# A Mamba block with its feed-forward layer on one core: two output products moved behind the last masked product, the first half's statistics on ScalarE, the bias added by GpSimd

## The chip, the cores and the metric

The kernel runs on one core of one Trainium2 chip. The metric is the device time of one launch in microseconds (us), as the median of several runs. Before the change it is 1815.36 us.

## What is computed

The input is x, 1024 tokens by 512 channels, in float32. A row of six vectors (shift, scale and gate, twice) comes from a small conditioning product. Cut to what matters here:

```python
h = layernorm(x) * (1 + ca) + sa
x = x + ga * attn(h)          # Mamba-2: in_proj, conv, SSD over 128 heads, group norm, out_proj
h = layernorm(x) * (1 + cb) + sb
x = x + gb * (h @ sign(w_ffn).T + b_ffn)
```

In `attn`, the 8192 inner channels are normalised in 8 groups of 1024: `g = y * silu(gate)`, divided by the root of the mean of g squared over the group, then multiplied with `out_proj_w` and summed over all groups.

## The kernel before, in words

**Tiles and units.** Tokens are worked on in two halves of 512 (four chunks of 128). Inner channels are worked on in 16 blocks of 512 (8 heads). A unit is one block for one half. There are 32 units, numbered u; four of them (c = 0 to 3) make a group g, in the order block 0 half 0, block 0 half 1, block 1 half 0, block 1 half 1. The last unit (g = 7, c = 3, `end` in the code) is followed by a tail: the output products of the last unit, the second layernorm, and the feed-forward product.

**Order of work.** Everything is written out by hand in five instruction streams (SyncE, TensorE, ScalarE, VectorE, GpSimd), with semaphores between them; the program order of each engine is the order of the code. No scheduler moves anything.

**One unit.** TensorE makes the gate projection, transposes the convolved x (`transposes`, L745), makes chunk states (`states`, L667), and, in the first part of unit u, the output products of unit u-1 (`out_proj(u - 1, z)`, four of them, z = 0 to 3, each of 12 matmuls 128x512 on lines 492 to 494, into banks 4 and 5 in turn). Then come four steps j, of two heads each: `exp_a` (L698) and `diff` (L681) are the products that ScalarE turns into decays (L1137, L1129, L1132); VectorE multiplies the decays with the masked C·B matrix (`mix`, L1517); TensorE makes Y_off (L819) and the masked product Y_diag (L836); VectorE adds the skip and scales Y_off (L1542, L1547); GpSimd adds and gates (L1734, L1737); ScalarE rounds the gated tile to its high part and squares it (`split_g`, L1149, L1156); VectorE makes the low part (`lower_g`, L1524); GpSimd sums the squares (`add_squares`, L1729). The last masked product is L836 of j = 3.

**Output products and the accumulator.** VectorE's `accumulate` reads an output product from its bank and adds the partial sum that a DMA brought (L1430), in the last unit and the tail multiplies by the gate row ga (L1433), and adds it, scaled by the group's inverse root, to `acc`, the residual stream (L1439). The products of u = 30, made in the last unit, complete the first half of `acc` (tiles 0 to 3). The products of u = 31, made in the tail, complete tiles 4 to 7.

**The second layernorm and the feed-forward layer.** At the end of the last unit VectorE takes mean and variance of tiles 0 to 3 (L1275, L1277) ahead of its last `lower_g`. In the tail ScalarE normalises (`normalise`, L1222), TensorE transposes (`turn`, L862), ScalarE scales and shifts the transposed tile and rounds it (`to_h`, L1242, L1244), VectorE makes the low part (`low`, L1591). The statistics of tiles 4, 5 and 6 are two passes on ScalarE (`stats`, L1227, L1229), those of tile 7 VectorE's. For each token tile t TensorE adds the bias as two products of one row (`bias`, L867, L868) and makes eight matmuls (`ffn`, L873); VectorE multiplies by gb and adds to `acc` (`y`, L1598, L1600); SyncE stores the tile.

The program prints the functions that the change touches here:

## Time and profile before

| what | value |
|---|---|
| median of 3 runs | 1815.36 us (1815.17 to 1816.68) |
| the profiled execution's own time | 1818.66 us |
| its span, first to last instruction | 1816.8 us |
| TensorE busy | 1744.9 us, 96% |
| VectorE busy | 1287.3 us, 71% |
| ScalarE busy | 1026.3 us, 56% |
| GpSimd busy | 946.0 us, 52% |
| mean granted TensorE clock | 0.989 of full speed |

Times in the trace are microseconds from the start of the span. A row of a timeline gives the start, the duration, the engine, the line, the operation, the tile written and the tiles read; in square brackets, how long the engine had been idle before it and which instruction ended that. "x2" means two such instructions merged in one row. Matmuls overlap, so one row's duration is longer than the distance to the next.

### The profile page before, as it was taken

The numbers are of one execution on the slowest core, as the hardware profiler recorded it, in microseconds if no ns is written. First come the engines' busy times: TensorE is split into PE (matmuls) and PEld (weight loads), VectorE is DVE, ScalarE is ACT, GpSimd is POOL, SyncE is SP. The second block draws the span as 40 slices with busy tenths as digits, with TensorE's granted clock in tenths as the row PEclk, the third lists the DMA queues.
The fourth block names the chain that finished last, engine by engine and source line by source line (L and its number), as shares of the span: only waits on it lengthen the run. The fifth ranks groups of instructions, "written<-read, shape, count | busy, mean of one in ns | idle before, by whom it ended". The sixth has DMA issues, their size and how long they took to land.

```text
span 1816.8 us, 31172 instructions
## 1 busy us (share of the span) xinstructions
PE 1744.9 (96%) x9672; PEld 1331.0 (73%) x9672; DVE 1287.3 (71%) x2154; ACT 1026.3 (56%) x1732; POOL 946.0 (52%) x732
## 2 busy tenths in 40 slices
PE   6889999999999999999999999999999999999968
PEld 4567778777777777777777777777777777877756
DVE  4766677767766678766777677666787667876776
ACT  6556555665546556565555655465564655556544
POOL 1445464555535565354645555455653546666651
PEclk9899999999999999999999999999999999999989
DMA  6312121121212121021211212121210212212111
GB/s 228 105 35 73 56 71 47 44 61 54 73 29 73 50 71 52 26 73 56 69 50 37 67 49 79 29 73 48 67 58 27 73 56 67 71 49 67 56 47 58
DMA packets 80789, 112.44 MB, mean 62 GB/s; under 512 B 28385, under 2 KB 32481, under 8 KB 79842
## 3 DMA queue, kind: packets, MB, share of 16 engines
q1 hardware_dynamic: 62754, 77.71, 14.5%
q10 hardware_dynamic: 17856, 32.51, 5.3%
q8 instruction: 91, 1.49, 0.4%
q14 instruction: 88, 0.72, 0.1%
HBM read 87.90 MB, written 22.29 MB: 61 GB/s over the span
## 4 chain that ended last, share of the span: by engine, by line
issue 48%; POOL 35%; PE 9%; ACT 3%; DVE 2%; DMA 1%; SPq 1%; POOLq 1%; ACTq 0%; DVEq 0%
POOL yt L1734 10%; POOL ssq L1729 7%; POOL prev L1713 5%; POOL wg_lo L1639 4%; POOL wo_lo L1639 3%; POOL yt L1737 3%; POOL wx_lo L1639 2%; PE bank L492 2%; PE bank L494 2%; PE bank L493 2%; PE bank L667 1%; PE bank L873 1%; PE bank L745 1%; POOL acc L1659 1%; POOL acc L1657 0%
## 5 line engine op out<-in xcount | busy, mean ns | idle before, releaser
L1734 POOL TENSOR_TENSOR yt<-yt,ea 128x384 f32<-128x384 f32 (+1 forms) x128 | 189.5, 1480 | 386.4 <-DVE ea L1547 386.4
L1517 DVE TENSOR_TENSOR lm<-lm,cbm 128x512 f32<-128x512 f32 x256 | 189.4, 781 | 161.5 <-ACT lm L1132 161.4
L1328 DVE SCALAR_TENSOR_TENSOR xc<-bank,bpar,xc 128x511 f32<-128x511 f32 (+2 forms) x384 | 286.2, 745 | 6.8
L492 PE MATMUL bank<-h_hi,wg_hi 128*128 128x512 f32 x640 | 262.7, 410 | 21.3 <-ACT gate L1078 11.1
L494 PE MATMUL bank<-h_hi,wg_lo 128*128 128x512 f32 x640 | 251.5, 393 | 0.0
L493 PE MATMUL bank<-h_lo,wg_hi 128*128 128x512 f32 x640 | 250.5, 391 | 0.0
L492 PE MATMUL bank<-h_hi,wx_hi 128*128 128x512 f32 x512 | 211.3, 413 | 2.3 <-DVE bt L1328 2.3
L492 PE MATMUL bank<-wo_hi,g_hi 128*128 128x512 f32 x496 | 206.6, 417 | 0.0
L494 PE MATMUL bank<-h_hi,wx_lo 128*128 128x512 f32 x512 | 201.7, 394 | 0.0
L493 PE MATMUL bank<-h_lo,wx_hi 128*128 128x512 f32 x512 | 200.7, 392 | 0.0
L494 PE MATMUL bank<-wo_hi,g_lo 128*128 128x512 f32 x496 | 194.8, 393 | 0.0
L1713 POOL TENSOR_TENSOR prev<-prev,dec 128x512 f32<-128x512 f32 x96 | 102.2, 1064 | 175.4 <-DVE prev L1471 110.2
L493 PE MATMUL bank<-wo_lo,g_hi 128*128 128x512 f32 x496 | 193.3, 390 | 0.0
L1078 ACT ACTIVATE gate<-bank 128x512 f32<-128x512 f32 x128 | 75.2, 587 | 207.2 <-PE bank L494 83.6
L1137 ACT ACTIVATE ea<-bank 128x512 f32<-128x512 f32 x128 | 76.5, 598 | 187.6 <-PE bank L698 139.9
L1737 POOL TENSOR_TENSOR yt<-yt,gate 128x512 f32<-128x512 f32 x128 | 165.6, 1294 | 10.0
L492 PEld LDWEIGHTS bank<-h_hi,wg_hi 128*128 128x128 f32 x640 | 120.8, 189 | 64.3 <-DVE xc L1328 14.6
L948 ACT ACTIVATE xc<-bank,bpar 128x512 f32<-128x512 f32 (+1 forms) x128 | 99.2, 775 | 112.9 <-PE bank L494 63.5
L1132 ACT ACTIVATE lm<-lm 128x512 f32<-128x512 f32 x256 | 148.9, 644 | 0.0
L1639 POOL TENSOR_TENSOR wx_lo<-raw_w,wx_hi 128x512 fp32r<-128x512 f32 x64 | 87.3, 1369 | 118.4 <-ACT wx_hi L918 118.4
L836 PE MATMUL bank<-lm,xdt 128*64 128x128 f32 x2048 | 140.9, 280 | 4.0 <-DVE lm L1517 2.0
L1729 POOL TENSOR_TENSOR ssq<-ssq,sq 128x512 f32<-128x512 f32 x112 | 144.4, 1290 | 0.0
(210 smaller groups left out, 3712.7 us busy)
## 6 DMA issues: line engine op xcount, KB each, us to landing
raw_w<-w_in_dram SPq DMA_DIRECT2D x145, 256.0 KB, 2.7
raw_w<-w_out_dram SPq DMA_DIRECT2D x64, 256.0 KB, 2.6
part_d<-part ACTq DMA_DIRECT2D x64, 256.0 KB, 2.4
part<-part_d ACTq DMA_DIRECT2D x60, 256.0 KB, 2.7
rt<-rows_d SPq DMA_DIRECT2D x256, 6.0 KB
acc<-x_dram SPq DMA_DIRECT2D x8, 256.0 KB, 6.6
acc<-w_mod_dram SPq DMA_DIRECT2D x2, 1024.0 KB, 6.0
lh<-neg_d SPq DMA_DIRECT2D x128, 6.0 KB
```

Source lines behind the costliest of these rows:

```text
L492: nc.tensor.matmul(out_ap, whi(k), hhi(k), start=(k == 0), stop=False)
L493: nc.tensor.matmul(out_ap, whi(k), hlo(k), start=False, stop=False)
L494: last = nc.tensor.matmul(out_ap, wlo(k), hhi(k), start=False, stop=(k == n - 1))
L836: lst = nc.tensor.matmul(bank[yd_bank(end, j)][64 * i:64 * i + 64, chunk(z)], xdt[:, z, h * HDIM:(h + 1) * HDIM], lm[:, h % 4, chunk(z)], ...
L1132: act(lm[:, h % 4, :], lm[:, h % 4, :], ACT.Exp, scale=-1.0).then_inc(a_l, 1)
L1328: stt(dst[:, at], ps[:, 0:HALF - 3 + k], w(k), dst[:, at], ALU.mult, ALU.add)\
L1517: tt(lm[:, h % 4, :], lm[:, h % 4, :], cbm[:, toks(hf)], ALU.mult).then_inc(v_m, 1)
L1639: tt(lo[:, j, :], raw_w[:, s, :], hi[:, j, :].bitcast(F), ALU.subtract).then_inc(p_w, 1)
L1713: tt(prev[:, slot(hf, z + 1), :].rearrange("p (h c) -> p h c", h=BH), prev[:, slot(hf, z), :].rearrange("p (h c) -> p h c", h=BH), d.unsqu ...
L1729: tt(ssq[:, hf, :], ssq[:, hf, :], sq[:, :], ALU.add).then_inc(p_ss, 1)
L1734: tt(yt[:, j % 2, cols], yt[:, j % 2, cols], ea[:, j % 2, cols], ALU.add).then_inc(p_t3, 1)
L1737: tt(yt[:, j % 2, :], yt[:, j % 2, :], gate[:, j, :], ALU.mult).then_inc(p_g, 1)
```

## The change

It has five parts, all in the last unit and the tail.

1. **Output products.** In the last unit TensorE makes `out_proj(30, 2)` and `out_proj(30, 3)` behind the last masked product, not ahead of the first decays. VectorE's `accumulate` for them moves with them: z = 2 stands behind its last L1547 and ahead of the low part of j = 2, z = 3 ahead of the low part of j = 3. SyncE's loads of the partial sums wait for these.
2. **First half's statistics.** VectorE's four means and variances at the end of the last unit are gone. ScalarE makes them in two passes per tile (`stats(0)` to `stats(3)`): two tiles between its work for j = 2 and for j = 3, two behind j = 3. VectorE scales the sums in one small instruction in the tail (`variance`), behind the group's sum. Tiles 6 and 7 are VectorE's now (`own_stats`), tiles 4 and 5 remain ScalarE's.
3. **Tail order.** TensorE transposes tiles 0 to 3 behind `out_proj(31, 2)`, where it was behind `out_proj(31, 1)`. VectorE adds the third accumulator tile ahead of the first two low parts, and the fourth, with `own_stats(6)` and `own_stats(7)`, ahead of the other two. ScalarE normalises tiles 4 to 7 behind all four `to_h` of the first half. The feed-forward product of tiles 0 and 1 is interleaved by k, as that of 4 and 5 already was.
4. **Bias.** The two one-row products per token tile are gone. GpSimd multiplies the bias, loaded to all 128 partitions, by gb once in the last unit, and adds it to each tile of `acc` when that tile has been normalised (`add_bias`); VectorE's last addition waits for it. The two ScalarE copies that split the bias row are gone.
5. **Squares.** In the last unit the squares of odd j go to a buffer of their own, and GpSimd adds those of j = 1 and j = 2 behind the gating of j = 3.

The core of the diff:

```diff
 TensorE, last unit
                     if z == 3:
-                        if not first:
+                        if not first and not end:
                             out_proj(u - 1, 2, None, (g, c))
                         states(2)
                         exp_a(0)
                         diff(0)
                         diff(1)
-                    if not first:
+                    if not first and not (end and z == 3):
 TensorE, tail
+            te.wait_ge(a_ea, 4 * UNITS)
+            out_proj(u - 1, 2, None, (GROUPS - 1, 3))
+            te.wait_ge(v_t2, 4 * u + 3)
+            out_proj(u - 1, 3, None, (GROUPS - 1, 3))
+            out_read(GROUPS - 1, 3, 2)
             out_proj(u, 0, None, (GROUPS, 0))
             sum_squares(GROUPS - 1, 1)
+            out_read(GROUPS - 1, 3, 3)
             out_proj(u, 1, None, (GROUPS, 0))
+            out_proj(u, 2, None, (GROUPS, 0))
             te.wait_ge(a_fall, 8 * UNITS)
             for t in range(NZ):
                 turn(t)
-            out_proj(u, 2, None, (GROUPS, 0))
             out_proj(u, 3, None, (GROUPS, 0))
-            te.wait_ge(p_bias, 1)
...
+            ffn_tiles(0, 1)
+            te.wait_ge(ln_sems[1]["a_n"], NK)
+            turn(4)
+            turn(5)
+            out_read(GROUPS, 0, 2)
+            ffn_tiles(2)
+            turn(6)
+            turn(7)
+            out_read(GROUPS, 0, 3)
+            ffn_tiles(3)
+            te.wait_ge(v_y, 2)
+            ffn_tiles(4, 5)
+            te.wait_ge(v_y, 3)
+            ffn_tiles(6)
+            te.wait_ge(v_y, 4)
+            ffn_tiles(7)
 ScalarE
+            def stats(t):
+                se.wait_ge(v_acc, 4 * (UNITS - 2) + t + 1)
+                act(xw[:, 0, :], acc[:, t, :], ACT.Identity, scale=-1.0 / HID, accum_out=nmr[:, t:t + 1]).then_inc(a_st, 1)
+                se.wait_ge(a_st, 2 * t + 1)
+                act(xw[:, 1, :], acc[:, t, :], ACT.Square, bias=nmr[:, t:t + 1], accum_out=mv[:, t, 1:2]).then_inc(a_st, 1)
...
+                    if j == 3 and not more:
+                        se.wait_ge(t_st, states_before(NBLK, 0))
+                        stats(0)
+                        stats(1)
 VectorE, last unit
+                    if end and j == 3:
+                        accumulate(u, g1, b1, h1, 2, end)
                     if j >= 1:
                         lower_g(j - 1)
...
                 if end:
-                    for t in range(NZ):
-                        ve.wait_ge(v_acc, 4 * (UNITS - 2) + t + 1)
-                        token_stats(ln_sems[1], t, acc_tile)
...
-                    half_var(ln_sems[1], 0)
+                    accumulate(u, g1, b1, h1, 3, end)
                 lower_g(NCT - 1)
 GpSimd
+            def add_bias(t):
+                po.wait_ge(a_xn, t + 1)
+                tt(acc[:, t, :], acc[:, t, :], bias_row, ALU.add).then_inc(p_bias, 1)
+            norm_pair(slice(0, NZ), 1)
+            po.wait_ge(p_gbias, 1)
+            add_bias(0)
+            norm_pair(slice(4, 5), 2)
+            for t in range(1, NZ):
+                add_bias(t)
+            norm_pair(slice(5, 6), 3)
+            po.wait_ge(v_neg, 1)
+            norm_pair(slice(6, 7), 4)
+            po.wait_ge(v_neg, 2)
+            norm_pair(slice(7, 8), 5)
+            for t in range(NZ, NT):
+                add_bias(t)
```

Line numbers of VectorE's instructions shift with the change (L1430, L1433, L1439 become L1445, L1448, L1459, and L1524 becomes L1544).

The first place is VectorE at the end of the last unit. `bank0` and `bank7` are the two products of j = 3; `wx_lo` holds the low parts of the gated tiles of this unit; `part` and `acc` are those of `accumulate`. Before:

```order
L1542 SCALAR_TENSOR_TENSOR yt<-xc,bpar,bank0 128x512
L1547 TENSOR_TENSOR ea<-bank7,ea 128x512
L1524 SCALAR_TENSOR_TENSOR wx_lo<-yt,bpar,wx_hi 128x512
L1275 BN_STATS bn<-acc 128x6
L1277 BN_AGGR mv<-bn 128x2
```

The pair of L1275 and L1277 stands there four times, and after it two small instructions and the last low part. With the change:

```order
L1562 SCALAR_TENSOR_TENSOR yt<-xc,bpar,bank0 128x512
L1567 TENSOR_TENSOR ea<-bank7,ea 128x512
L1445 TENSOR_TENSOR part<-bank4,part 128x512
L1448 TENSOR_TENSOR part<-part,rows 128x512
L1459 SCALAR_TENSOR_TENSOR acc<-part,rstd,acc 128x512
L1544 SCALAR_TENSOR_TENSOR wx_lo<-yt,bpar,wx_hi 128x512
L1445 TENSOR_TENSOR part<-bank5,part 128x512
L1448 TENSOR_TENSOR part<-part,rows 128x512
L1459 SCALAR_TENSOR_TENSOR acc<-part,rstd,acc 128x512
L1544 SCALAR_TENSOR_TENSOR wx_lo<-yt,bpar,wx_hi 128x512
```

The four statistics are gone, and the two accumulations stand one ahead of each of the last two low parts.

The second place is ScalarE at the end of the last unit, from the high part of j = 2 to the normalising of the first half. Before:

```order
L1149 ACTIVATE wx_hi<-yt,bpar 128x512 [waits p_g]
L1156 ACTIVATE sq<-yt 128x512 [waits p_ss]
L1149 ACTIVATE wx_hi<-yt,bpar 128x512 [waits p_g]
L1156 ACTIVATE sq<-yt 128x512 [waits p_ss]
L1222 ACTIVATE xc<-acc,nmr,rs 128x512 [waits p_nmr,v_t2]
```

With the change:

```order
L1158 ACTIVATE wx_hi<-yt,bpar 128x512 [waits p_g]
L1169 ACTIVATE sq<-yt 128x512 [waits p_ss]
L1100 ACTIVATE xw,nmr<-acc 128x512 [waits v_acc,t_st]
L1102 ACTIVATE xw,mv<-acc,nmr 128x512 [waits a_st]
L1100 ACTIVATE xw,nmr<-acc 128x512 [waits v_acc]
L1102 ACTIVATE xw,mv<-acc,nmr 128x512 [waits a_st]
L1158 ACTIVATE wx_hi<-yt,bpar 128x512 [waits p_g]
L1169 ACTIVATE ssq<-yt 128x512 [waits p_ss]
```

Two tiles' statistics stand ahead of the last high part; the other two follow the last row shown.

The third place is VectorE in the tail, ahead of the third and fourth low part of the first half (`h_lo`). Before:

```order
L1430 TENSOR_TENSOR part<-bank4,part 128x512
L1433 TENSOR_TENSOR part<-part,rows 128x512
L1439 SCALAR_TENSOR_TENSOR acc<-part,rstd,acc 128x512
L1591 TENSOR_TENSOR h_lo<-lm,h_hi 128x512 x2
L1581 TENSOR_SCALAR rs<-mv 128x1
```

With the change:

```order
L1445 TENSOR_TENSOR part<-bank5,part 128x512
L1448 TENSOR_TENSOR part<-part,rows 128x512
L1459 SCALAR_TENSOR_TENSOR acc<-part,rstd,acc 128x512
L1594 TENSOR_SCALAR rs<-mv 128x1
L1284 BN_STATS bn<-acc 128x6
L1286 BN_AGGR mv<-bn 128x2
L1601 TENSOR_SCALAR nmr<-mv 128x1
L1602 TENSOR_SCALAR rs<-mv 128x1
```

The last four of these stand there twice, and then come the two `h_lo`: the fourth accumulation (`bank5`) and both tiles' statistics are now ahead of them, where only the third accumulation was.

## Rows read from the trace of the kernel before

**Rows 1.** The page: span, and TensorE's busy time.

```profile
span 1816.8 us, 31172 instructions
PE 1744.9 (96%) x9672; PEld 1331.0 (73%) x9672; DVE 1287.3 (71%) x2154; ACT 1026.3 (56%) x1732; POOL 946.0 (52%) x732
```

**Rows 2.** Stretches: start:end, length, each engine's busy us, PEclk, DMA share.

```profile
1760.40:1769.90 9.50, 0.07 (x2) 0.00 (x0) 7.42 (x16) 2.88 (x5) 8.91 (x7) 0.69 0.01 2
1769.90:1774.00 4.10, 4.03 (x10) 3.20 (x11) 0.01 (x1) 2.76 (x4) 2.33 (x3) 0.50 0.00 0
...
1785.80:1798.80 13.00, 11.98 (x48) 8.08 (x47) 8.07 (x17) 6.81 (x13) 3.18 (x6) 0.87 0.11 42
```

**Rows 3.** Who waited for whom, 1725 to 1817: total, times, longest.

```profile
PE bank L492 <- DVE wx_lo L1524: 9.5, 1, 9.5
```

**Rows 4.** Timeline of TensorE: start, duration, instruction.

```profile
1742.12 0.50 PE L492 MATMUL bank<-wo_hi,g_hi 128*128 128x512 f32 x1
...
1759.37 1.09 PE L836 MATMUL bank<-lm,xdt 128*64 128x128 f32 x16 [1.37 <-DVE lm L1517]
1769.97 0.80 PE L492 MATMUL bank<-wo_hi,wx_hi 128*128 128x512 f32 x1 [9.50 <-DVE wx_lo L1524]
...
1775.59 0.47 PE L492 MATMUL bank<-wo_hi,wx_hi 128*128 128x512 f32 x1
...
1778.45 1.91 PE L862 MATMUL bank<-ident,xc 128*128 128x128 f32 x16
...
1785.77 0.49 PE L867 MATMUL bank<-wg_hi 1*128 1x512 f32 x1
...
1797.79 1.03 PE L862 MATMUL bank<-ident,prev 128*128 128x128 f32 x8
...
1810.16 0.49 PE L867 MATMUL bank<-wg_hi 1*128 1x512 f32 x1
...
1810.82 0.50 PE L873 MATMUL bank<-wg_lo,h_hi 128*128 128x512 f32 x1
```

**Rows 5.** Timeline of VectorE.

```profile
1741.05 0.69 DVE L1430 TENSOR_TENSOR part<-bank,part 128x512 f32<-128x512 f32 x1 [1.70 <-PE bank L494]
...
1747.67 1.29 DVE L1517 TENSOR_TENSOR lm<-lm,cbm 128x512 f32<-128x512 f32 x2
...
1750.29 2.36 DVE L1517 TENSOR_TENSOR lm<-lm,cbm 128x512 f32<-128x512 f32 x2
...
1764.50 0.98 DVE L1524 SCALAR_TENSOR_TENSOR wx_lo<-yt,bpar,wx_hi 128x512 fp32r<-128x512 f32 x1 [1.78 <-ACT wx_hi L1149]
1765.40 0.68 DVE L1275 BATCH_NORM_STATS2 bn<-acc 128x6 f32<-128x512 f32 x1
...
1788.62 0.69 DVE L1591 TENSOR_TENSOR h_lo<-lm,h_hi 128x512 fp32r<-128x512 f32 x1 [0.64 <-ACT h_hi L1244]
...
1813.67 0.69 DVE L1600 TENSOR_TENSOR acc<-acc,ea 128x512 f32<-128x512 f32 x1
```

**Rows 6.** Two lines of VectorE, 1570 to 1817: ns shortest/median/longest, first and last start.

```profile
L1430 DVE TENSOR_TENSOR part<-bank,part x12: 676/688/692, 1579.4 to 1789.3; 128x512 f32<-128x512 f32 x12
L1439 DVE SCALAR_TENSOR_TENSOR acc<-part,rstd,acc x12: 752/752/1723, 1580.7 to 1790.7; 128x512 f32<-128x512 f32 x12
```

**Rows 7.** Timeline of ScalarE.

```profile
1746.50 1.15 ACT L1132 ACTIVATE lm<-lm 128x512 f32<-128x512 f32 x2
...
1771.24 2.93 ACT L1222 ACTIVATE xc<-acc,nmr,rs 128x512 f32<-128x512 f32 x4 [1.41 <-POOL nmr L1746]
1778.17 0.63 ACT L1227 ACTIVATE ssq<-acc 128x512 f32<-128x512 f32 x1 [4.00 <-DVE acc L1439]
...
1780.07 0.78 ACT L1242 ACTIVATE lm<-bank,modc 128x512 f32<-128x512 f32 x1 [0.33 <-PE bank L862]
```

**Rows 8.** Timeline of GpSimd.

```profile
1750.30 1.80 POOL L1734 TENSOR_TENSOR yt<-yt,ea 128x512 f32<-128x512 f32 x1 [9.17 <-DVE ea L1547]
...
1767.90 1.27 POOL L1729 TENSOR_TENSOR ssq<-ssq,sq 128x512 f32<-128x512 f32 x1
```

More of the change, by code:

```diff
@@ L278, in ea_bank, with square @@
             return 4 if j else gate_bank(c, 2)
+        def square(end, j):
+            return ssq[:, 0, :] if end and j % 2 else sq[:, :]
         def yo_bank(end, j):
@@ L827, in unit @@
                         else:
-                            out_read(g, c, 3)
+                            out_read(g, c, 1 if end else 3)
                     else:
@@ L1497, in unit @@
                         tt(by_head(xw[:, z % 2, :]), src, heads(dtw[:, hf], 1, z), ALU.mult).then_inc(v_xw, 1)
-                    if z == 3 and not first:
-                        accumulate(u, g1, b1, h1, 2, end)
+                    if z == 3 and not first and not end:
+                        accumulate(u, g1, b1, h1, 2)
                     if z >= 1:
@@ L1528, in unit @@
                 mix(1)
-                if not first:
-                    accumulate(u, g1, b1, h1, 3, end)
+                if not first and not end:
+                    accumulate(u, g1, b1, h1, 3)
                 if hf == 0:
@@ L1728, in add_squares @@
                         ge(po, p_ss, squares_before(g, c) + j - (c < 2))
-                    tt(ssq[:, hf, :], ssq[:, hf, :], sq[:, :], ALU.add).then_inc(p_ss, 1)
+                    tt(ssq[:, hf, :], ssq[:, hf, :], square(last and c == 3, j), ALU.add).then_inc(p_ss, 1)
                 for j in range(NCT):
@@ L1737, in unit @@
                     tt(yt[:, j % 2, :], yt[:, j % 2, :], gate[:, j, :], ALU.mult).then_inc(p_g, 1)
-                    if j >= (2 if c < 2 else 1):
+                    if last and c == 3:
+                        for k in ((), (0,), (), (1, 2))[j]:
+                            add_squares(k)
+                    elif j >= (2 if c < 2 else 1):
                         add_squares(j - 1)
```

144 lines of the change are left out of this document (60 added, 84 removed).

## The prediction

> **What bounds the kernel now.** I read the page first: TensorE is busy 1744.9 of 1816.8 us [rows 1], so over 31 units it is the bound, and the change touches none of them. All of it lies behind 1738 us, so I read only that stretch, engine by engine. There TensorE is not the bound. Between its last masked product (L836, 1759.37 plus 1.09) and the first output product of u = 31 (1769.97) it does nothing for 9.5 us [rows 3, 4]: it waits for the last low part, L1524. Ahead of that stands a chain through all engines: VectorE's L1547, GpSimd's add and gate, ScalarE's high part, VectorE's low part. GpSimd is busy 8.91 of 9.50 us in this pause, VectorE 7.42 [rows 2]. After it the granted clock is 0.50 [rows 2], the lower of the two levels, for 4.1 us. The reader should see three milestones. **S** is the start of the first product of u = 31: 1769.97 [rows 4]. **L** is the end of the fourth low part of the first half: 1788.62 + 0.69 = 1789.31 [rows 5]. **T** is the end of the last transposes: 1797.79 + 1.03 = 1798.8 [rows 4]. Behind T a fixed chain runs to VectorE's last addition at 1813.67 [rows 5], and the store. I give each part as a shift of these.
>
> **The last unit's heads.** Removed: an output product is 12 matmuls, 1775.59 to 1778.45, 2.85 us [rows 4]. One stood ahead of the first decays, one from 1742.12 [rows 4] ahead of the second pair's. VectorE idled 1.70 us for the first one (1741.05) and spent about 2.1 us on each accumulation (0.69 + 0.69 + 0.75) [rows 5, 6]. Without them, ScalarE's own queue is next: its second pair of exponentials (1746.50 [rows 7]) can start when the first pair is done, which I put 2.9 us earlier. VectorE's second pair of masks (1747.67 [rows 5]) is then 3.4 us earlier, GpSimd's first add (1750.30 [rows 8]) too. In the middle steps some of it is lost to the next effect; the last masked product (1759.37) I put at 1756.25, 3.1 us earlier.
>
> **The end of the last unit, the largest term.** What L1517 shows is important: two masks take 1.29 us, but 2.36 us when GpSimd is adding (its L1734 from 1750.30 took 1.80, not 1.27) [rows 5, 8]. The low part at 1764.50 took 0.98 [rows 5]. L1430, which reads a bank, never takes over 692 ns, L1439, which reads two tiles, up to 1723 [rows 6]. So VectorE's instructions with two tiles as inputs and GpSimd's take turns. The Trainium skill, page "SBUF — State Buffer", section "SBUF: two separate sides", says so: a shared port pair is an exclusive lock for the whole instruction. The trace agrees, and it is a rule that speaks against this change. By that rule the sum below is as it stands; with no lock it would be the first rival's.
>
> From GpSimd's gating of j = 2, which ends at 1760.6 by the shifts above, there remain five GpSimd instructions of 1.25 us (add and gate of j = 3, three sums of squares; 1.27 in [rows 8] less the overlap) and, new, six of VectorE with two tiles, 0.62 each: two times multiply, accumulate, low part. Before, only two of these six stood there; the rest was statistics of one input (L1275, 0.68 [rows 5]). Taking turns: 5 x 1.25 + 6 x 0.62 = 9.95, so the low part ends at 1770.55 and S = 1770.65, **0.7 us later**. The 3.1 us are spent. Bounds: with no turns at all, ScalarE decides. High part of j = 2 to 1761.25, square 0.55, two tiles of statistics at 1.55 each (to 1764.9; L1227 is 0.63 [rows 7], and the other pass and the two reads bring it to 1.55), high part, low part: S = 1766.2. If the two moved products run at the lower clock (0.43 a matmul, 5.2 us each), the accumulations start later: S = 1771.3. I take the turns, because the rows show them at each overlap.
>
> **S to the fourth product.** Before 1769.97 to 1785.77, 15.8 us [rows 4], 1.8 us of them for the low clock behind the pause (nine matmuls 0.2 us slower). The pause is now 5.7 to 7.6 us, so I leave that in. The transposes, 1.91 us [rows 4], are only moved by one product: the fourth normalised tile comes just then. Again 15.85: **no shift**. But ScalarE's first `to_h` comes later. It was at 1780.07, S + 10.1 [rows 7]. Now: the group's sum at S + 5.6, VectorE's `variance` behind its first multiply at S + 6.4, GpSimd's two powers, four tiles in 2.93 [rows 7] to S + 11.7, `stats(4)` to S + 13.3, two `to_h` of 1.35 to S + 16.0.
>
> **The low parts in the tail.** L was S + 19.35. Now VectorE makes the second low part to S + 16.65, then accumulates the fourth tile (2.15), makes the statistics of tiles 6 and 7 (about 1.05 each: 0.68 [rows 5] and three small ones), and only then the third and fourth low part (1.3): S + 22.2. Beside it GpSimd makes three bias additions of 1.27 [rows 8], each of which can hold VectorE once; none to two full waits give 0 to 2.1, I take 1.0. L = S + 23.2, **3.85 us later** against S. Each accumulator addition also stands in front of its `own_stats`; TensorE, with its fourth product done and half of the two-tile product made, waits some 5 us for the third low part, and its clock can fall again.
>
> **L to T.** Before 9.5 us, with 3.4 us at the low clock (0.87 mean over 1785.8 to 1798.8 [rows 2]): two matmuls, a bias pair, eight matmuls, eight transposes, a bias pair, eight matmuls, eight transposes. Now four matmuls (1.0), eight transposes (1.03 [rows 4]), eight matmuls (2.1: from 1810.82 to the last addition's product [rows 4, 5]), eight transposes: 5.1 at the full clock, 6.6 if the pause brought it down. I take 5.9: **3.6 us earlier**.
>
> **Behind T.** The chain is `to_h`, low parts, y(3), low parts, then three tiles' products. Two bias pairs are on it, each 1810.82 - 1810.16 = 0.66 [rows 4]: **1.3 us earlier**. The four later bias additions of GpSimd are done before y needs them.
>
> **Edits that cost nothing.** The bias times gb on GpSimd (1.27) takes the place of the one-row subtraction, in the 9.17 us that GpSimd idles there [rows 8]; the bias load to all partitions has 25 us. The two copies that ScalarE loses stood in front of a wait for TensorE. If GpSimd's cover went, its first add would be 1.3 later at most.
>
> **Sum.** 0.7 + 0 + 3.85 - 3.6 - 1.3 = -0.35, with 0.05 for the longer 15.85: -0.3 us. On the profiled execution that is 1818.66 to 1818.4; its span is 1816.8 and 1.86 lie around it. The median is 3.3 below the profiled time; I put the same difference on it: 1815.36 - 0.3 = **1815.1 us**. A measurement of this kernel can tell about 0.2%, 3.6 us, from no change.
>
> **Rivals.** (1) *No turns at the end of the last unit.* S = 1766.2, -3.8; L = S + 22.2, +2.85; L to T 5.1, -4.4; behind T -1.3; together -6.6: 1808.8. For it: the moved products come when GpSimd has much of its work behind it, and some turns fall into VectorE's waits for a bank. Against: 8.91 of 9.50 us busy [rows 2]. (2) *The clock stays up at S*, since TensorE now works in the middle of the pause: -1.8 on top of the forecast, 1813.3. (3) *Slower: the third low part becomes the wait.* Its place is VectorE's queue in the tail: fourth accumulation and two tiles' statistics ahead of low parts for which TensorE waits. With full waits there (L = S + 24.3, +4.95), S at 1771.3 (+1.3), the clock low through all that follows (L to T 7.6, -1.9) and no gain behind T but 0.8, together 1.3 + 4.95 - 1.9 - 0.8 = +3.55, 1818.9. It decides from where L comes over 6.3 us later than 1789.3. For it: all four products are done and nothing else is left for TensorE. Against: it takes all bounds at once. (4) *Nothing reaches the end, since the moved products only fill the pause*, is the forecast itself.
>
> **Chances.** Forecast 0.47, (1) 0.24, (2) 0.16, (3) 0.13. Forecast and (2) are within 0.2%, (1) is faster, (3) slower: 0.24, 0.63, 0.13. The range reaches from (1) to (3), less their far ends: 1808.5 to 1819.0.
>
> **What the profile will show.** Right: the last masked product about 3 us earlier, TensorE's two moved products behind it, L1448, L1459 and L1544 at 1 to 1.9 us instead of 0.7 there, S within 1 us of 1770.6; then a pause of 4 to 6 us in the two-tile product, ended by a low part; T near 1799.7; no L867. Wrong: S below 1768, or these three lines at their short times (rival 1); L over 1796 (rival 3); or a bias addition as the releaser of the last additions.

## The result, and the profile after

The change makes the kernel slower by a little: 1818.96 us median of 20 runs (1817.68 to 1823.54), where the kernel before had 1816.03 us of 20 runs beside it (1814.93 to 1819.3). The ratio is 1.0017, 95% interval 1.0011 to 1.0024: 2.0 to 4.4 us slower. The forecast was 1815.1, a little faster. The median lies just inside the range of 1808.5 to 1819.0, but the time moved the other way. The profiled execution took 1820.51 us, with this span:

```profile
span 1818.7 us, 31171 instructions
...
PE 1740.0 (96%) x9656; PEld 1329.5 (73%) x9656; DVE 1292.5 (71%) x2148; ACT 1029.0 (57%) x1742; POOL 956.5 (53%) x740
```

TensorE does 4.9 us less and the kernel is slower, so all of it is a matter of waits. What TensorE waited for from 1735 us on (total, times, longest):

```profile
PE bank L871 <- DVE h_lo L1612: 7.4, 5, 5.0
PE bank L494 <- issue: 5.8, 1, 5.8
PE bank L838 <- DVE lm L1537: 4.2, 1, 4.2
```

The 9.5 us of [rows 3] are now 5.8: the two moved products stand right behind the last masked product, and the pause follows them. The view names no releaser for it ("issue"); VectorE's last low part ends 0.1 us before the pause does. But 4.2 us stand ahead of the last masked product, where it was 1.37 [rows 4], and 5.0 us ahead of a feed-forward matmul in the tail. In the kernel before, the low parts cost TensorE this much there:

```profile
PE bank L873 <- DVE h_lo L1591: 1.4, 4, 0.6
```

**Milestones from an anchor.** The part of the run ahead of the last unit differs by up to 3 us between the profiled executions, also where the code there is the same. So I count from the start of GpSimd's first decay of the last unit, at 1730.90 in the kernel before. In the changed kernel it is this row:

```profile
1730.50 1.19 POOL L1734 TENSOR_TENSOR prev<-prev,dec 128x512 f32<-128x512 f32 x1
```

All rows of the table are us from that instruction, of one profiled execution each. S is the start of the first output product of u = 31, L the end of the fourth low part, T the end of the last transposes, as in the prediction. One of the 11 executions of e2_lows_first took 2824.7 us, at a mean granted clock of 0.559, and its ratio leaves that one out.

| kernel | last masked product | S | L | T | last addition | end of span | median, us | before beside it | ratio, 95% interval |
|---|---|---|---|---|---|---|---|---|---|
| before | 28.47 | 39.07 | 58.41 | 67.92 | 82.77 | 85.90 | | | |
| the change | 27.25 | 41.38 | 64.90 | 71.97 | 85.08 | 88.20 | 1818.96 | 1816.03 | 1.0017 (1.0011 to 1.0024) |
| e1_products_back | 28.48 | 38.95 | 63.46 | 71.08 | 85.71 | 88.89 | 1819.35 | 1815.26 | 1.0019 (1.0010 to 1.0028) |
| e2_lows_first | 27.23 | 41.38 | 63.02 | 69.64 | 83.45 | 86.62 | 1816.64 | 1815.26 | 1.0006 (0.9997 to 1.0016) |
| e3_six_more | 26.39 | 40.52 | 64.26 | 71.46 | 84.58 | 87.70 | 1818.3 | 1815.26 | 1.0017 (1.0008 to 1.0026) |
| e4_bias_alone | 28.47 | 39.07 | 59.99 | 67.12 | 82.70 | 85.80 | 1815.99 | 1815.26 | 1.0004 (0.9995 to 1.0013) |
| f2_bias_in_gaps | 28.47 | 39.07 | 58.74 | 66.43 | 79.56 | 82.72 | 1814.04 | 1816.7 | 0.9986 (0.9977 to 0.9995) |
| f3_bias_in_gaps_two_tiles | 28.47 | 39.07 | 58.74 | 65.87 | 78.94 | 82.04 | 1814.54 | 1816.7 | 0.9989 (0.9980 to 0.9998) |
| g1_no_bias_additions | 27.25 | 41.36 | 63.42 | 71.35 | 86.02 | 89.14 | 1819.83 | 1816.7 | 1.0018 (1.0009 to 1.0027) |
| g2_short_sums | 26.39 | 39.14 | 63.49 | 71.05 | 84.13 | 87.28 | 1818.76 | 1816.7 | 1.0012 (1.0003 to 1.0021) |
| h1_tail_order_alone | 28.47 | 39.06 | 60.53 | 71.53 | 86.37 | 89.46 | 1821.47 | 1815.22 | 1.0034 (1.0022 to 1.0046) |
| h2_gaps_and_squares | 28.48 | 39.14 | 58.84 | 65.97 | 79.09 | 82.18 | 1812.6 | 1815.22 | 0.9985 (0.9976 to 0.9994) |
| h3_gaps_two_tiles_squares | 28.47 | 39.14 | 59.01 | 66.14 | 79.21 | 82.30 | 1812.99 | 1815.22 | 0.9990 (0.9981 to 0.9999) |
| i1_lows_first_no_bias | 26.39 | 40.52 | 61.22 | 67.66 | 80.77 | 83.89 | 1815.19 | 1815.68 | 0.9994 (0.9985 to 1.0003) |

For the change the table reads: last masked product 1.2 earlier; from there to S 14.1 instead of 10.6, so that S is 2.3 later; S to L 23.5 instead of 19.3, **+4.2**; L to T 7.1 instead of 9.5, **-2.4**; T to the last addition 13.1 instead of 14.9, **-1.7**. With the 2.3 by which S is late, the end is +2.3, beside +2.9 of the medians.

**The last unit.** TensorE's clock, in the changed kernel (columns as in [rows 2]):

```profile
1736.00:1741.00 5.00, 3.48 (x15) 1.41 (x13) 3.64 (x6) 3.13 (x6) 2.28 (x2) 1.00 0.26 68
1741.00:1747.60 6.60, 6.50 (x34) 4.69 (x35) 3.94 (x6) 4.96 (x11) 0.02 (x1) 0.50 0.21 70
```

With the two products gone TensorE is busy 3.48 of 5.00 us, and then the granted clock is 0.50, its lower level, for 6.6 us. The kernel before had 1.00 over these 6.6 us, but it has a stretch at the lower level of its own in the same unit, later:

```profile
1754.00:1756.00 2.00, 2.00 (x16) 1.77 (x17) 1.23 (x1) 2.00 (x4) 1.92 (x2) 0.50 0.00 0
```

It cost nothing there: e1_products_back and e4_bias_alone, whose clock stayed at 1.00 in that stretch, have their last masked product at the same 28.47 and 28.48. The changed kernel's TensorE, VectorE and GpSimd (a timeline of each, put together):

```profile
1748.34 2.73 DVE L1537 TENSOR_TENSOR lm<-lm,cbm 128x512 f32<-128x512 f32 x2 [0.84 <-ACT lm L1141]
...
1754.27 3.42 DVE L1537 TENSOR_TENSOR lm<-lm,cbm 128x512 f32<-128x512 f32 x2 [1.28 <-ACT lm L1141]
...
1754.20 1.27 POOL L1758 TENSOR_TENSOR yt<-yt,gate 128x512 f32<-128x512 f32 x1
1755.42 1.72 POOL L1750 TENSOR_TENSOR ssq<-ssq,sq 128x512 f32<-128x512 f32 x1
...
1757.75 1.72 PE L838 MATMUL bank<-lm,xdt 128*64 128x128 f32 x16 [4.20 <-DVE lm L1537]
```

The last two masks take 3.42 us with two GpSimd instructions beside them, and the last masked product waits for them. Two masks alone take 1.29 [rows 5]; the last two in the kernel before took this:

```profile
1757.53 1.79 DVE L1517 TENSOR_TENSOR lm<-lm,cbm 128x512 f32<-128x512 f32 x2 [1.72 <-ACT lm L1132]
```

**The end of the last unit**, VectorE and then GpSimd:

```profile
1763.40 0.69 DVE L1445 TENSOR_TENSOR part<-bank,part 128x512 f32<-128x512 f32 x1 [2.31 <-PE bank L496]
1764.13 1.15 DVE L1448 TENSOR_TENSOR part<-part,rows 128x512 f32<-128x512 f32 x1
1765.32 1.66 DVE L1459 SCALAR_TENSOR_TENSOR acc<-part,rstd,acc 128x512 f32<-128x512 f32 x1
1766.90 1.75 DVE L1544 SCALAR_TENSOR_TENSOR wx_lo<-yt,bpar,wx_hi 128x512 fp32r<-128x512 f32 x1
1768.58 0.68 DVE L1445 TENSOR_TENSOR part<-bank,part 128x512 f32<-128x512 f32 x1
1769.29 1.04 DVE L1448 TENSOR_TENSOR part<-part,rows 128x512 f32<-128x512 f32 x1
1770.37 0.75 DVE L1459 SCALAR_TENSOR_TENSOR acc<-part,rstd,acc 128x512 f32<-128x512 f32 x1
1771.03 0.75 DVE L1544 SCALAR_TENSOR_TENSOR wx_lo<-yt,bpar,wx_hi 128x512 fp32r<-128x512 f32 x1
```

```profile
1764.70 1.73 POOL L1750 TENSOR_TENSOR ssq<-ssq 128x512 f32<-128x512 f32 x1
1766.57 1.53 POOL L1750 TENSOR_TENSOR ssq<-ssq,sq 128x512 f32<-128x512 f32 x1
1768.25 1.53 POOL L1750 TENSOR_TENSOR ssq<-ssq 128x512 f32<-128x512 f32 x1
```

Read the starts across both fences: 1764.70 (GpSimd), 1765.32 with 1.66 (VectorE), 1766.57, 1766.90 with 1.75, 1768.25, 1769.29. They come in turns, and each of the four stretched VectorE instructions with two tiles as inputs (L1448 twice, L1459, L1544) ends about 0.6 after a GpSimd one. L1445, which reads a bank, is 0.68 throughout. Once GpSimd is done, L1459 and L1544 are back at 0.75. This is the turn-taking that the prediction counted on. It adds some 2.7 us to VectorE's eight instructions (their lengths here less 0.69 or 0.75 each). But they also start late: the first waits 2.31 us for the moved product (first row), whose first matmul took 0.80 us, at the lower clock, where an output product's took 0.50 in [rows 4].

**The tail.** TensorE, then VectorE and GpSimd:

```profile
1771.88 0.77 PE L494 MATMUL bank<-wo_hi,wx_hi 128*128 128x512 f32 x1 [5.79 <-issue]
...
1794.86 0.80 PE L871 MATMUL bank<-wg_lo,h_hi 128*128 128x512 f32 x1 [4.97 <-DVE h_lo L1612]
...
1801.44 1.03 PE L864 MATMUL bank<-ident,prev 128*128 128x128 f32 x8
```

```profile
1789.27 1.07 DVE L1448 TENSOR_TENSOR part<-part,rows 128x512 f32<-128x512 f32 x1
1790.37 1.64 DVE L1459 SCALAR_TENSOR_TENSOR acc<-part,rstd,acc 128x512 f32<-128x512 f32 x1
...
1792.00 0.68 DVE L1284 BATCH_NORM_STATS2 bn<-acc 128x6 f32<-128x512 f32 x1
...
1794.12 1.28 DVE L1612 TENSOR_TENSOR h_lo<-lm,h_hi 128x512 fp32r<-128x512 f32 x2
...
1786.32 5.14 POOL L1787 TENSOR_TENSOR acc<-acc,cbm 128x512 f32<-128x512 f32 x3
```

TensorE stands still for 4.97 us until the third low part, which VectorE makes behind the fourth accumulation (with turns against three bias additions) and behind the statistics of two tiles, 2.1 us. The clock in that pause and behind it, and then that of the kernel before at about the same place of the tail:

```profile
1789.90:1794.90 5.00, 0.04 (x1) 0.04 (x1) 4.83 (x13) 4.01 (x6) 3.60 (x6) 0.73 0.00 0
1794.90:1799.20 4.30, 4.30 (x13) 3.42 (x14) 1.78 (x3) 0.87 (x2) 4.22 (x6) 0.52 0.00 0
```

```profile
1792.00:1794.00 2.00, 2.00 (x6) 1.41 (x6) 1.90 (x7) 0.00 (x0) 1.17 (x2) 0.50 0.02 4
```

So the clock fell in the kernel before too, where no wait was over 0.6 us; that it was the pause which brought it down in the changed kernel is not shown.

### The profile page after: what moved, and what is told of

The parts are those of the page before. It is cut to its first block, busy times and chain, and to the rows that moved or that the text cites. A ratio compares the mean times of both kernels' runs of the same rounds, so it can differ in the third digit from the quotient of the medians.

```text
span 1818.7 us, 31171 instructions
## 1 busy us (share of the span) xinstructions
PE 1740.0 (96%) x9656; PEld 1329.5 (73%) x9656; DVE 1292.5 (71%) x2148; ACT 1029.0 (57%) x1742; POOL 956.5 (53%) x740
## 4 chain that ended last, share of the span: by engine, by line
issue 48%; POOL 34%; PE 9%; ACT 3%; DVE 3%; DMA 1%; SPq 1%; POOLq 1%; ACTq 0%; DVEq 0%
POOL yt L1755 10%; POOL ssq L1750 7%; POOL prev L1734 5%; POOL wg_lo L1660 4%; POOL wo_lo L1660 3%; POOL yt L1758 3%; POOL wx_lo L1660 2%; PE bank L494 2%; PE bank L496 2%; PE bank L495 2%; PE bank L669 1%; PE bank L747 1%; PE bank L871 1%; POOL rstd L1716 0%; DMA gate<-w_mod_dram 0%
## 5 line engine op out<-in xcount | busy, mean ns | idle before, releaser
L494 PEld LDWEIGHTS bank<-h_hi,wg_hi 128*128 128x128 f32 x640 | 120.6, 188 | 66.2 <-DVE xc L1337 14.4
```

What stands on the lines that cost most here:

```text
L494: nc.tensor.matmul(out_ap, whi(k), hhi(k), start=(k == 0), stop=False)
```

## The experiments

Two theories stood at the start. **A**: the loss sits in the last unit (no work for TensorE, low clock, turns, S late). **B**: it sits in the tail, between S and L. Each expectation was written before its run.

### e1_products_back: part 1 undone in the changed kernel

```diff
-                        if not first and not end:
+                        if not first:
                             out_proj(u - 1, 2, None, (g, c))
...
-                    if not first and not (end and z == 3):
+                    if not first:
```

VectorE's accumulations, the loads and the waits for banks go back with them.

> The changed kernel with its first part alone undone: the third and fourth output product of the unit ahead, their two accumulations and the loads of the partial sums stand where they stood before. The rest of the change stays. The changed kernel's median is 2.9 us above the kernel before. Theory A (moving the products costs: the granted clock falls to the lower level behind 1741, and in the pause the two accumulations take turns with GpSimd): the time falls to about 1.5 us below the kernel before or better, the clock stays at the upper level from 1738 to 1750, and the first product of the last unit starts at 1766 to 1768, since neither statistics nor accumulations stand ahead of the last low part. Theory B (the loss is in the tail, where the fourth accumulation and two tiles' statistics stand ahead of the third and fourth low part): the time stays 2 to 3 us above the kernel before and only the start of the products moves.

Measured: 1819.35 us, ratio 1.0019, as slow as the change (1.0017). The clock stayed at 1.00 to 1758 us and S went back to 38.95, but L only to 63.46: S to L is 24.5 us. Against the changed kernel S is 2.4 us earlier, L 1.4, T 0.9, and the end 0.7 later. Behind T the clock was this, where the changed kernel had 1.00:

```profile
1810.00:1812.00 2.00, 2.00 (x6) 1.53 (x5) 1.42 (x3) 0.00 (x0) 0.00 (x0) 0.50 0.00 0
```

Eight matmuls of the last tiles start 0.43 us apart there and not 0.23, some 1.5 us by an estimate from TensorE's rows there. Even without them the kernel would gain under 1 of its 2.3 us: A is out as the main cause. Nor does S reach the 1766 to 1768 of theory A; it is at 1769.66. Two of the 11 executions took 1815.4 and 1815.6 us and the other nine 1818.5 and more, which stays unexplained. What holds S now is ScalarE, whose last high part stands behind two tiles of statistics (VectorE):

```profile
1768.36 1.25 DVE L1538 SCALAR_TENSOR_TENSOR wx_lo<-yt,bpar,wx_hi 128x512 fp32r<-128x512 f32 x1 [3.06 <-ACT wx_hi L1152]
```

### e2_lows_first: statistics of tiles 6 and 7 behind the low parts

```diff
-            own_stats(6, 0)
-            own_stats(7, 1)
             low(2)
             low(3)
+            own_stats(6, 0)
+            own_stats(7, 1)
```

> The changed kernel with one swap on VectorE in the tail: the third and fourth low part of the first half stand ahead of the statistics of tiles 6 and 7, not behind them. Theory B (they are what TensorE waits for in its 4.97 us pause): the fourth low part ends 2.1 us earlier, the pause shrinks to about 2.9 us, and the time falls by 1.5 to 3 us, to about that of the kernel before; if the clock then stays up, by 3 or more. Theory A (the loss is made in the last unit): under 1 us, because the last transposes then wait for the normalising of tiles 6 and 7.

Measured: 1816.64 us, ratio 1.0006, by this swap alone. That is 2.3 us less than the change by the medians, 2.0 by the ratios and 1.6 from the anchor. S to L went from 23.52 to 21.64. VectorE:

```profile
1789.92 1.28 DVE L1612 TENSOR_TENSOR h_lo<-lm,h_hi 128x512 fp32r<-128x512 f32 x2
...
1794.41 1.66 DVE L1622 TENSOR_TENSOR acc<-acc,ea 128x512 f32<-128x512 f32 x1
```

The low parts follow L1459 at once. The second row is the next cost: `y` now meets the later bias additions, and its addition takes 1.66 us instead of 0.69; T to the last addition is 13.81, 0.7 more than in the change.

### e3_six_more: six matmuls of no use, to keep TensorE busy in the last unit

```diff
                         diff(0)
                         diff(1)
+                        if end:
+                            out_read(g, c, 0)
+                            for _ in range(6):
+                                nc.tensor.matmul(bank[4][:, :], g_hi[:, 0, 0:128], wo_hi[:, 0, :], start=True, stop=True)
```

> The changed kernel with six added matmuls of 128x512 on TensorE behind the first decays' products, into a bank that is free there; nothing reads their result. Theory A1 (the moved products had kept TensorE busy, and without them the granted clock falls to the lower level from 1741 to 1747.6 in the changed kernel): the clock stays up there, the first masked product of the last unit starts as early or earlier although 1.4 us of work is added, and the last masked product starts 1 to 1.5 us earlier. The time falls by 0.5 to 1.5 us. Theory A2 (only the turns between VectorE and GpSimd matter): the last masked product is not earlier, the time is the same or up to 0.5 us longer.

Measured: 1818.3 us. The ratio, 1.0017, is that of the change, so the median shows no gain. From the anchor: the clock stayed at 1.00, the last masked product and S came 0.86 earlier, the end 0.5. So this low clock costs 0.9 us at S and 0.5 at the end. That the six matmuls kept it up is **not shown**: it also stayed up, without them, in g2_short_sums and in i1_lows_first_no_bias, whose stretch is this (compare 0.50 and 6.50 us busy above):

```profile
1741.00:1747.60 6.60, 5.43 (x53) 3.92 (x53) 4.23 (x7) 6.09 (x13) 0.87 (x1) 1.00 0.19 69
```

### e4_bias_alone: part 4 alone, in the kernel before

The two one-row products go, and GpSimd adds tiles 0 to 3 behind the group's root and 4 to 7 at its end.

```diff
             group_rstd(GROUPS - 1, 1)
+            po.wait_ge(p_gbias, 1)
+            for t in range(NZ):
+                add_bias(t)
...
+            for t in range(NZ, NT):
+                add_bias(t)
```

> The kernel before with the bias part alone: the bias times the gate row on GpSimd, added to each tile of the accumulator there, the sixteen one-row matmuls and ScalarE's two copies gone; the additions of tiles 0 to 3 behind GpSimd's group root, those of tiles 4 to 7 at its end. Forecast of the record: two pairs of 0.66 behind the last transposes and two ahead of them on the chain, 2.6 us faster than the kernel before, less up to 1 us where the first additions make VectorE's accumulations wait. Rival: GpSimd's additions hold up VectorE's accumulations and last additions as much as TensorE gains, no change within 0.5 us.

Measured: 1815.99 beside 1815.26 us: no gain from eight pairs of products less. GpSimd's two runs of four and VectorE's low parts beside them:

```profile
1774.50 6.52 POOL L1750 TENSOR_TENSOR acc<-acc,cbm 128x512 f32<-128x512 f32 x4
...
1793.42 6.83 POOL L1750 TENSOR_TENSOR acc<-acc,cbm 128x512 f32<-128x512 f32 x4
...
1779.79 2.38 DVE L1578 TENSOR_TENSOR h_lo<-lm,h_hi 128x512 fp32r<-128x512 f32 x2
...
1796.21 2.88 DVE L1578 TENSOR_TENSOR h_lo<-lm,h_hi 128x512 fp32r<-128x512 f32 x2 [0.52 <-ACT h_hi L1231]
```

Two low parts take 2.38 and 2.88 us instead of 0.69 each. L to T gains 2.4, S to L loses 1.6, and T to the last addition is 0.7 longer though two pairs less stand on it. Behind T the clock had fallen here too:

```profile
1804.00:1806.00 2.00, 2.00 (x5) 1.57 (x6) 0.96 (x2) 0.00 (x0) 0.00 (x0) 0.50 0.00 0
```

As in e1, some eight matmuls are 0.2 us further apart, about 1.5 us by the same estimate. So only a part of what is lost behind T is turns.

### f2_bias_in_gaps and f3_bias_in_gaps_two_tiles: the same additions at other places

```diff
+            po.wait_ge(p_gbias, 1)
+            for t in range(3):
+                add_bias(t)
             group_rstd(GROUPS - 1, 1)
...
-            for t in range(NZ, NT):
-                add_bias(t)
+                for b in ((3, 4), (5,), (), (6, 7))[z]:
+                    add_bias(b)
```

The lines are the main ones, against e4, whose four additions behind the root go too. Theory **C**: an addition costs nothing where VectorE waits or has the accumulator's first step, which reads a bank. f3 also interleaves the feed-forward product of tiles 0 and 1 by k, as the change does.

> The kernel before with the bias part, as in the run of the bias alone, but with GpSimd's eight additions where VectorE has no instruction with two tiles as inputs: those of tiles 0 to 2 ahead of GpSimd's last group root, in its idle time while TensorE makes the first product of the last unit; those of tiles 3 and 4 behind the normalising factors of tile 4, that of 5 behind those of 5, those of 6 and 7 at the end. Theory C (the bias part's gain of 2.6 us on TensorE was given back where the additions and VectorE took turns): from the start of the products to the fourth low part 19.4 us as before, not 20.9; behind the last transposes 13.5 to 14 us and not 15.6; 2.5 to 3.5 us faster than the kernel before. Rival D (TensorE's bias products were hidden, or the shorter work only lets its clock fall): no change within 0.5 us, wherever the additions stand.

> The run before this one with one more piece of the change: the feed-forward products of tiles 0 and 1 interleaved by k. Behind the fourth low part stand then four matmuls of this pair and not ten: six of 0.23 us, 1.4 us, come off the way to the last transposes. Theory C: 1 to 1.4 us faster than the run before this one, some 4 to 5 us faster than the kernel before. Rival D: the pause ahead of the third low part grows by as much and the clock falls, no change against the run before this one.

Measured: f2 is faster than both kernels, 1814.04 us beside 1816.7, ratio 0.9986 (0.9977 to 0.9995); T to the last addition is 13.13. The end is 3.1 us earlier than in e4, though not all of that is turns: behind T the clock stayed at 1.00, and about 1.5 us of the 3.1 is that (from e4's rows above). f3 has 1814.54, ratio 0.9989. Its L to T is 0.56 shorter and its end 0.7 earlier, but the medians don't tell the two apart, and the 1 to 1.4 us that theory C gave it did not come. GpSimd in f2:

```profile
1771.81 3.75 POOL L1749 TENSOR_TENSOR acc<-acc,cbm 128x512 f32<-128x512 f32 x3
...
1784.78 2.96 POOL L1749 TENSOR_TENSOR acc<-acc,cbm 128x512 f32<-128x512 f32 x2
```

Three additions take 3.75 us here, 1.25 each, where three took 5.14 in the change: GpSimd pays for the turns as well. VectorE idles 6.2 us between its last low part and the group's sum, and they lie there.

### g1_no_bias_additions: the changed kernel without the eight additions

The output lacks the bias, and the time is to be read without that work.

> The changed kernel with GpSimd's eight bias additions and the waits for them left out: the output lacks the bias. It measures what they cost in the tail. Theory C: VectorE's multiply and accumulate there are at 0.69 and 0.75 us again (1.07 and 1.64 to 1.76 in the changed kernel), from the start of the products to the fourth low part 21.5 to 22.2 us and not 23.5, VectorE's additions at the end at 0.69; 2 to 3 us faster than the changed kernel. Rival (they are hidden, as the forecast had it for those of tiles 4 to 7): under 1 us.

Measured: 1819.83 us, ratio 1.0018, no gain. L1448, L1459 and the last additions are back at 0.69 and 0.75 in the tail, S to L is 1.5 us shorter; but L to T is 7.93, 0.9 more, and T to the last addition 14.67, 1.6 more. The clock behind T, g1 first and then the changed kernel over the same stretch:

```profile
1808.00:1812.00 4.00, 3.75 (x10) 2.62 (x10) 2.79 (x5) 0.00 (x0) 0.00 (x0) 0.62 0.00 0
```

```profile
1808.00:1812.00 4.00, 3.24 (x13) 2.36 (x14) 3.11 (x5) 0.00 (x0) 0.00 (x0) 1.00 0.14 54
```

What was won at L was given back behind it, most of it at the lower clock behind T. That is no consequence of the missing additions that these runs show: e1 and e4 make them, and their clock fell at the same place. The theory that the turns with the bias additions alone are the 2 to 3 us fell.

### g2_short_sums: the sums of squares of j = 1 and 2 cut to 8 columns

```diff
-                    tt(ssq[:, hf, :], ssq[:, hf, :], square(last and c == 3, j), ALU.add).then_inc(p_ss, 1)
+                    n = 8 if last and c == 3 and j in (1, 2) else HALF
+                    tt(ssq[:, hf, 0:n], ssq[:, hf, 0:n], square(last and c == 3, j)[:, 0:n], ALU.add).then_inc(p_ss, 1)
```

Most of these sums is left out.

> The changed kernel with two of GpSimd's sums of squares at the end of the last unit cut from 512 to 8 columns (part of the squares is not summed, for the last group of the second half). It tests the taking of turns there. If turns set the start of the products of the last unit (forecast's largest term): two GpSimd instructions of 1.25 us are some 1 us shorter each, VectorE's 1.15, 1.66, 1.75 and 1.04 us for multiply, accumulate, low part and multiply fall towards 0.7, and the products start 1.5 to 2.5 us earlier. If ScalarE's two tiles of statistics ahead of the last high part set it, or the moved products themselves (they end at 1766.0), the start moves under 0.7 us.

Measured: S at 39.14, 2.24 earlier, of which 0.86 is the clock (last masked product at 26.39, as in e3). The other 1.4 come from the two short GpSimd instructions (0.65 instead of 1.53 to 1.73) and the turns that went with them, a little under the 1.5 to 2.5 that was expected of turns; VectorE:

```profile
1763.05 0.75 DVE L1544 SCALAR_TENSOR_TENSOR wx_lo<-yt,bpar,wx_hi 128x512 fp32r<-128x512 f32 x1
```

The end moved by only 0.9 and the median not measurably (1818.76, ratio 1.0012 with an interval that overlaps that of the change): an earlier S is not an earlier end while the tail has its own waits.

### h1_tail_order_alone: part 3 alone, in the kernel before

```diff
             out_proj(u, 1, None, (GROUPS, 0))
+            out_proj(u, 2, None, (GROUPS, 0))
             te.wait_ge(a_fall, 8 * UNITS)
             for t in range(NZ):
                 turn(t)
-            out_proj(u, 2, None, (GROUPS, 0))
...
+            second(2)
+            variance(4)
             low(0)
             low(1)
-            variance(4)
-            second(2)
+            second(3)
+            variance(5)
             low(2)
             low(3)
-            variance(5)
-            second(3)
```

> The kernel before with the tail order of part 3 alone: the transposes of tiles 0 to 3 behind the third product, VectorE's third accumulation ahead of the first two low parts and the fourth ahead of the other two. S and everything ahead of it as before (39.1 us from the start of GpSimd's first decay of the last unit). Theory D (the tail's order is what costs, whoever makes the statistics): the first to_h comes later by about the third accumulation, 2.1 us, and the third low part by the fourth; S to L 22 to 23.5 instead of 19.3, L to T 7 to 8 instead of 9.5 since a product's wait is gone, end +1 to +2 us. Rival (only the statistics of tiles 6 and 7 ahead of the low parts and the turns with the bias additions cost, the order is free): S to L under 21, end within 0.5 us of before.

Measured: 1821.47 us, ratio 1.0034, slower than the change itself. From the anchor it is 3.6 us at the end; the rest of the 6.2 between the medians lies ahead of the anchor, where this edit changes nothing, and stays unexplained. So the 3.6 are the measure of this edit and not the ratio. S to L is 21.47, +2.1. ScalarE's first `to_h` and TensorE:

```profile
1782.24 0.78 ACT L1242 ACTIVATE lm<-bank,modc 128x512 f32<-128x512 f32 x1 [3.04 <-PE bank L862]
```

```profile
1789.29 0.50 PE L873 MATMUL bank<-wg_lo,h_hi 128*128 128x512 f32 x1 [2.24 <-DVE h_lo L1591]
...
1792.51 0.79 PE L873 MATMUL bank<-wg_lo,h_hi 128*128 128x512 f32 x1
```

`to_h` starts at S + 13.1 instead of S + 10.1: the transposes themselves are short (1.91 us [rows 4]), but the chain of `to_h` and low parts starts from them, and it now starts one product later. ScalarE idles 3.04 us for them, TensorE then 2.24 us for the third low part, and its matmuls are 0.79 long, at the lower clock, so that L to T grows to 11.0. Neither number was met: theory D had 22 to 23.5 for S to L and the rival under 21. Theory D has the direction and the mechanism; that L to T would shrink was wrong.

### h2_gaps_and_squares and h3_gaps_two_tiles_squares: part 5 on top of f2 and f3

> f2_bias_in_gaps with part 5 (the squares of odd j in a buffer of their own, the sums of j = 1 and 2 behind the gating of j = 3). Theory E: in the kernel before GpSimd's sum of squares stands between its two gatings and holds the last low part, so S comes 1.0 to 1.3 us earlier (37.8 to 38.1 from the anchor) and the end 0.7 to 1.3 us, median 1812.8 to 1813.4. Rival (ScalarE's queue or VectorE's four statistics hold the last low part): S stays at 39.1 within 0.3, the median that of f2_bias_in_gaps.

> f3_bias_in_gaps_two_tiles with part 5. Theory E: S 1.0 to 1.3 us earlier than 39.1, end 3.5 to 5 us earlier than before in the anchored trace, median 1812.2 to 1813.2. Rival: S at 39.1, median 1814 to 1814.6.

Measured: S at 39.14 in both, so the rival was right, and the reason stands in two rows of h2, ScalarE's last high part and VectorE's last low part:

```profile
1766.55 0.72 ACT L1139 ACTIVATE wx_hi<-yt,bpar 128x512 fp32r<-128x512 f32 x1 [1.66 <-POOL yt L1732]
```

```profile
1769.16 0.74 DVE L1518 SCALAR_TENSOR_TENSOR wx_lo<-yt,bpar,wx_hi 128x512 fp32r<-128x512 f32 x1
```

The high part is done at 1767.3, but VectorE's four statistics are ahead of the low part until 1769.1. h2 is the fastest kernel measured here, 1812.6 us beside 1815.22, ratio 0.9985; f2 has 0.9986, so part 5 brings nothing that can be told. h3's median, 1812.99, lies in theory E's range, but with S unmoved that is no support for it: its ratio is 0.9990, and f3 had 0.9989. Putting the last low part ahead of the last two statistics was not tried.

### i1_lows_first_no_bias: e2 and g1 together

> The changed kernel with the third and fourth low part ahead of the statistics of tiles 6 and 7, and without GpSimd's eight bias additions (the output lacks the bias; the time is read without that work). S stays at 41.4 from the anchor. Theory F (the two costs of the tail are separate, and what is left of S to L is the tail's order, 21.5 us as in h1_tail_order_alone): S to L 21.4 to 21.8 less the turns that h1 did not have, no turn at L1448, L1459 or L1612, L to T 7 to 7.5, T to the last addition 13.1 to 14.7; end 2.5 to 4 us before that of the changed kernel, median 1815 to 1816.5. Rival (the clock gives it back again, as in g1_no_bias_additions): S to L as said, but T to the last addition over 14.5 and the median within 1 us of 1818.

Measured: 1815.19 us, 3.8 less than the change and 4.3 from the anchor, though e2 alone gave 2.3 (1.6 from the anchor) and g1 alone nothing. S to L is 20.70, L to T 6.44, T to the last addition 13.11. TensorE's wait of 4.97 us is this:

```profile
1790.46 0.50 PE L871 MATMUL bank<-wg_lo,h_hi 128*128 128x512 f32 x1 [1.59 <-DVE h_lo L1612]
...
1791.79 0.79 PE L871 MATMUL bank<-wg_lo,h_hi 128*128 128x512 f32 x1
```

Behind 1.59 us instead of 4.97 the first matmul takes 0.50 instead of 0.80: the clock had not fallen yet. It fell 1.3 us later (the 0.79), but for some 3 us only, where the change stood at the lower level to 1799. Theory F holds in its order of size. S to L is 0.7 less than it said, L to T 6.44 and not 7 to 7.5, the end 4.3 us earlier and not 2.5 to 4; S is 0.86 earlier, since the clock had stayed up in the last unit too. Of the +4.18 of S to L, e2 takes 1.9 and g1 1.5; the two together 2.8, and 1.4 are left. I put them on the order of the tail, which is 2.1 alone in h1; no run takes that order back in the changed kernel.

## Why the prediction was wrong, step by step

**"The last unit's heads": this step failed.** It put the last masked product 3.1 us earlier; it came 1.2 earlier. Two things were missed. Without the products the granted clock was 0.50 for 6.6 us; that is 0.86 us of the 1.9, by the runs in which it stayed up (e3, g2, i1). And the masks came to lie beside GpSimd: 2.73 and 3.42 us for two, where the kernel before had 2.36 and 1.79 and the step moved them at these lengths, with "some of it is lost" for the rest. That the masks are the other 1.0 is read from the rows; no run isolates it.

**"The end of the last unit, the largest term": the mechanism was right in part**, and it was the term that spoke against the change. From the last masked product to S it asked for 14.4 us and 14.1 were measured. The turns are there, in four of the six two-input rows, and g2 takes 1.4 us off with two of GpSimd's sums. But a part of the 14.1 is VectorE's wait of 2.31 us for the moved product, which the step had only as a bound, so that the close number is partly luck. (Its own terms give 9.97 and not 9.95, which changes nothing.) The Trainium skill, page "SBUF — State Buffer", section "SBUF: two separate sides", says that an instruction of VectorE with two inputs in SBUF and one of GpSimd that reads SBUF share an exclusive lock, and that the one that starts first holds it to its end. The rows agree: L1459 takes 1.66 beside GpSimd and 0.75 without. S came at 41.38 from the anchor and not at 39.75, because of the step ahead of it: 1.0 beyond the bound of 1771.3.

**"S to the fourth product" and "The low parts in the tail": right.** From S to the end of the fourth product 15.85 was predicted and 15.2 measured; L = S + 23.2 was predicted, 23.5 measured. What the step did not see is that this +4.2 was avoidable: e2, g1, i1 and h1 split it into statistics ahead of the low parts, turns, and order.

**"L to T": mis-sized.** Predicted 5.9, with 6.6 as its upper end; measured 7.1. The step knew that TensorE would wait some 5 us (4.97) and that its clock "can fall again", and then took a value halfway. It fell: 0.52 over the 4.3 us behind the pause, with seven matmuls behind L, 0.43 us apart, where the step had four at 0.25.

**"Behind T": right**, -1.7 for -1.3. But "the four later bias additions of GpSimd are done before y needs them" looks at the wrong cost: additions cost by turns, not by being late, as two low parts at 2.88 us in e4 show. In the changed kernel itself they made two additions of `y` 0.4 us longer each.

**The sum.** +1.6 at S, +0.3, +1.2 and -0.4 are 2.7 us on the forecast of -0.3, and give the measured +2.3 from the anchor within 0.1. So the steps that failed are the last unit's heads (1.6 of it at S) and L to T (1.2). But a late S alone is not why the kernel is slower: in e1 S is as before and the time is not. The third rival, "the third low part becomes the wait", came nearest: its decision point was L over 6.3 us later, L came 6.5 later from the anchor, though not over the 1796 that was named as its sign (1795.8 on that scale). That its 1818.9 meets the measured 1818.96 is luck: it adds 3.55 us to 1815.36 with every term off by 0.5 to 1.0 (S +1.3 for +2.3, L +4.95 for +4.2, L to T -1.9 for -2.4, behind T -0.8 for -1.7), and the kernel before had 1816.03 beside the change. It was given 0.13 because "it takes all bounds at once". The long pause needed no bound of S, however: e1 has the same 4.97 us with S at its old place.

## What to carry to other kernels

Where VectorE and GpSimd both read two tiles, cost each new instruction at the turn it forces on the other engine, and put it into a stretch in which the other one waits: the bias part with its eight additions was worth nothing at one place and 0.14% at another, a part of it through the clock. Ahead of an instruction for which the bounding engine waits stands nothing that can wait itself; one swap (e2) gave back most of the loss. Work taken from the bounding engine in a stretch that is set by latency buys less than its own length: two products of 2.85 us each brought the last masked product 1.2 us earlier, 2.1 where the clock stayed up. And a profile of one execution shows one course of the clock: look at the clock in the same stretch of both kernels before a difference is put down to an edit.

## What the runs showed of the hardware that was not expected

- The granted clock fell to 0.50 in the last unit although TensorE's longest idle times there were 0.65 and 0.96 us, and not in every kernel with the same pauses: in the change, e2 and g1 it fell (0.50 to 0.54), in e3, g2 and i1 it did not. It is the same some 23 to 27 us behind the anchor in the kernels that kept the products where they were: 0.50 in the kernel before, f2, f3 and h1, and 1.00 in e1, e4, h2 and h3, with the last masked product at 28.47 or 28.48 in all eight. One profiled execution of each can't say what decides.
- GpSimd pays for the turns too. An addition takes 1.25 us in f2's gap, and 1.63 to 1.71 on the mean in the change and in e4 (5.14 for three, 6.52 and 6.83 for four).
- The clock behind T is another such case: it fell in e1 (0.50 from 1810 to 1812), e4 (0.50 from 1804 to 1806) and g1 (0.62 from 1808 to 1812), and not in the other eleven kernels. By the estimate at e1 it is worth some 1.5 us, as much as several of these edits moved.
